# A decoder kernel: inverse softmax sums moved from VectorE to ScalarE in the first cross attention, weight scales moved into the linear attention

## What is computed

```python
x = x + gla(layernorm(x))
x = x + cross_attention(layernorm(x), ctx, ctx)      # the stage that is changed
x = x + attention_and_experts(layernorm(x))
x = x + t5_attention(layernorm(x)); x = x + similarity_attention(layernorm(x), ctx)
x = x + quantised_ffn(layernorm(x))                  # its weights are scaled by 127 / max|w|

# cross_attention: h = 16 heads, s = 77 keys
attn = softmax(einsum('bhtd,bhsd->bhts', q, k) * 8 ** -0.5)
out = einsum('bhts,bhsd->bhtd', attn, v).reshape(b, t, 128) @ out_w.T + out_b

# quantised_ffn, for each group of weights that share a scale
amax = clip(max(abs(w)), 1e-8); scale = 127 / amax
w_q = clip(round(w * scale), -128, 127) / scale
```

## Time and profile before

| what | us |
|---|---|
| median of 3 runs | 493.52 |
| the 3 runs | 493.2, 493.52, 498.61 |
| the profiled execution | 495.03 |
| span of the core in it | 493.2 |
| busy in the span: PE, DVE, ACT, POOL | 436.3, 373.3, 284.9, 212.8 |
| the cross attention, from the first scores to the last residual | 77.6 to 122.8 |

### The profile page before, as it was taken

The page is one execution under the profiler, slowest core; times in us unless marked ns, Lnnn a source line. Parts: engine busy times, 40 slices in busy tenths (PEclk is TensorE's granted clock), DMA queues, the critical chain, the costliest instruction groups (busy, mean ns, idle before and its releaser), DMA issues.

```text
span 493.2 us, 13018 instructions
## 1 busy us (share of the span) xinstructions
PE 436.3 (88%) x4488; PEld 303.9 (62%) x4488; DVE 373.3 (76%) x1005; ACT 284.9 (58%) x617; POOL 212.8 (43%) x542
## 2 busy tenths in 40 slices
PE   3879968887675899879999999999999998999897
PEld 1225555665573767746666676676676675887656
DVE  3746868998777699987777777778778777567666
ACT  2752324655328487567777777777777776413460
POOL 5050011270024265504685767667675776442200
PEclk9959988999999799999999999999999999999999
DMA  6388922600000012100000000000000000000001
GB/s 211 64 98 98 101 30 72 239 23 3 0 2 20 26 43 85 34 1 1 19 19 2 3 16 0 16 0 0 0 0 0 0 2 1 3 2 1 2 0 43
DMA packets 15619, 15.77 MB, mean 32 GB/s; under 512 B 1348, under 2 KB 12859, under 8 KB 15579
## 3 DMA queue, kind: packets, MB, share of 16 engines
q1 hardware_dynamic: 15579, 15.24, 15.1%
HBM read 10.52 MB, written 4.72 MB: 31 GB/s over the span
## 4 chain that ended last, share of the span: by engine, by line
PE 69%; DVE 22%; ACT 5%; issue 3%; DMA 1%; POOL 0%; SPq 0%; DVEq 0%; ACTq 0%; POOLq 0%
PE bank L922 16%; PE bank L1416 11%; PE bank L1368 9%; PE bank L1291 5%; PE bank L1218 4%; PE bank L1409 3%; PE bank L1205 3%; PE bank L1287 3%; PE bank L1306 2%; DVE PX L1716 2%; DVE mx L1714 2%; PE bank L1031 2%; PE bank L1528 1%; DVE stats L1555 1%; PE bank L1536 1%
## 5 line engine op out<-in xcount | busy, mean ns | idle before, releaser
L826 ACT ACTIVATE SN<-SN,nmx 128x512 f32<-128x512 f32 x128 | 92.7, 724 | 9.9 <-DVE nmx L1929 7.6
L922 PE MATMUL bank<-cs,SN 128*128 128x128 f32 x512 | 67.3, 274 | 3.3 <-DVE Z L1922 1.6
L922 PEld LDWEIGHTS bank<-cs,SN 128*128 128x128 f32 x512 | 57.1, 141 | 18.1 <-issue 12.1
L1368 PE MATMUL bank<-TK,TQ 64*128 64x512 f16 x384 | 52.6, 379 | 1.6 <-DVE TK L1892 1.6
L540 POOL TENSOR_TENSOR CTW<-YT 128x128 f32<-128x128 f32 x64 | 29.3, 458 | 51.5 <-DVE YT L1927 51.0
L1914 DVE CUSTOM_DVE_ANT_0 SN<-bank,strip 128x512 f32<-128x512 f32 x64 | 43.4, 677 | 1.2 <-PE bank L1368 0.6
L1929 DVE CUSTOM_DVE_ANT_0 SN<-bank,strip 128x512 f32<-128x512 f32 x64 | 43.6, 681 | 0.0
L1922 DVE COPY PTO<-bank 128x512 f32<-128x512 f32 x32 | 22.1, 692 | 21.0 <-PE bank L1416 20.9
L1922 DVE COPY Z<-bank 128x512 f32<-128x512 f32 x32 | 22.1, 691 | 16.0 <-PE bank L1416 15.9
L837 ACT COPY PTO<-bank 128x512 f32<-128x512 f32 x32 | 18.8, 586 | 26.1 <-PE bank L1416 26.1
L1416 PE MATMUL bank<-PTO,TV 128*64 128x128 f32 x512 | 33.4, 273 | 0.0
(11 more groups left out here) (314 smaller groups left out, 987.3 us busy)
## 6 DMA issues: line engine op xcount, KB each, us to landing
bias_rows<-biasr SPq DMA_DIRECT2D x1, 4096.0 KB, 44.4
band<-bias_rows SPq DMA_DIRECT2D x1, 3072.0 KB, 12.7
wqkv<-in_twqkv SPq DMA_DIRECT2D x8, 192.0 KB, 2.8
w1s<-in_w SPq DMA_DIRECT2D x8, 128.0 KB, 2.2
w2s<-in_w SPq DMA_DIRECT2D x8, 128.0 KB, 2.2
wB<-in_wb SPq DMA_DIRECT2D x1, 753.0 KB, 6.2
wA<-in_wa SPq DMA_DIRECT2D x1, 520.0 KB, 4.7
X<-in_x SPq DMA_DIRECT2D x2, 256.0 KB, 3.4
```

The costliest lines, as they stand in the source:

```text
L826: sc.activation(p, p, ACT.Exp, bias=nmx[:, r % RING, h:h + 1], scale=-1.0, accum_out=psm[:, r % RING, h:h + 1]).then_inc(sm["exp_ready"], 1)
L922: return nc.tensor.transpose(out_, in_, ident[0:n, 0:n])
L1368: ins = mm(bank[2 * (s % 2) + h][:, :], TQ[u][r, q_part, S * b + P * qt:S * b + P * qt + P], TK[u][r, k_part, S * b:S * b + S], start=(k = ...
```

## The change

Four edits. (1) The reciprocal of the sums leaves DVE. ACT makes it in a new function `inverse_sums(i)`: the logarithm of the sums from bank 6 into rc, then the exponential of minus that, which raises the new semaphore `rc_ready`. It is issued on ACT for tile i - 1 behind the exponential of tile i, and for tile 7 behind the loop, ahead of `rstd_of(3, 0)`. (2) The product that makes CT leaves its place ahead of `subtract_max(i + 1)` and stands inside it, between the maximum and the difference; the product of tile 6 stands behind the statistics of step 7, and that of tile 7 stays where it was. (3) `weight_scales` leaves the cross attention for the GLA loop, in three parts behind `gate_out` of tiles 0, 1 and 2, with its maximum split into two halves. (4) Semaphores `h1_mm` and `gl_mm` become one, `gk_mm`, counted on. What PE does, and in which order, is unchanged.

```diff
@@ -309,7 +309,7 @@
 
         names = """ld_x ld_cs ld_a ld_b ld_c ld_d bias_dma dve_c act_c qx_ready konst_ready
             ln_var ln_rstd ln_y ln_tp ln_yt x_done
-            qk_mm h1_mm h1_ready gl_mm u_ready l_ready g_ready e_ready kp_ready qs_ready kp_tp kpt_ready vg_mm vg_ready
+            qk_mm gk_mm h1_ready rc_ready u_ready l_ready g_ready e_ready kp_ready qs_ready kp_tp kpt_ready vg_mm vg_ready
             a_mm am_ready kv_mm st_ready o_mm ob_ready sq_ready ss_ready sr_ready og_ready ot_mm ot_ready go_mm
             kv_x_mm kb_ready kx_ready vx_ready vs_mm vb_ready qt_mm qt_hi qt_ready xb_ready s_mm px_sub px_ready pt_mm pt_ready xo_mm ct_ready ws_ready co_mm
             qkv_mm qkv_ready sc_ready se_ready at_pool at_ready att_mm att_ready pr_mm h2_ready rt_mm lg_ready le_ready xh_ready
@@ -627,7 +627,7 @@
                 take_yt(0, g)
 
             for g in range(NG):
-                act.wait_ge(sm["h1_mm"], g + 1)
+                act.wait_ge(sm["gk_mm"], g + 1)
                 sc.copy(H1[:, S * g:S * g + S], bank[4 + g][0:LR, :]).then_inc(sm["h1_ready"], 1)
             for g in range(NG):
                 c = slice(S * g, S * g + S)
@@ -701,9 +701,18 @@
             query_high(0)
             take_ot(1)
 
+            def inverse_sums(i):
+                act.wait_ge(sm["xo_mm"], i + 1)
+                if i >= 1:
+                    act.wait_ge(sm["ct_ready"], i)
+                link(sc.activation(rc[:, :], bank[6][:, P:2 * P], ACT.Ln))
+                sc.activation(rc[:, :], rc[:, :], ACT.Exp, scale=-1.0).then_inc(sm["rc_ready"], 1)
+
             for i in range(NT):
                 act.wait_ge(sm["px_sub"], i + 1)
                 sc.activation(PX[:, i % 2, :, :], PX[:, i % 2, :, :], ACT.Exp, scale=XD ** -0.5).then_inc(sm["px_ready"], 1)
+                if i >= 1:
+                    inverse_sums(i - 1)
                 if i == NT - 1:
                     rstd_of(2, 0)
                 if i == 1:
@@ -717,6 +726,7 @@
                         rstd_of(1, 1)
                     if i == 1 and c == 1:
                         query_high(1)
+            inverse_sums(NT - 1)
             rstd_of(3, 0)
 
 
@@ -952,10 +962,10 @@
             pe.wait_ge(sm["ld_a"], 48)
             for g in range(NG):
                 pe.wait_ge(sm["ln_yt"], g + 1)
-                mm(bank[4 + g][0:LR, :], wA_("gk1", LR), YT[:, S * g:S * g + S], start=True, stop=True).then_inc(sm["h1_mm"], 1)
+                mm(bank[4 + g][0:LR, :], wA_("gk1", LR), YT[:, S * g:S * g + S], start=True, stop=True).then_inc(sm["gk_mm"], 1)
             for g in range(NG):
                 pe.wait_ge(sm["h1_ready"], g + 1)
-                mm(bank[4 + g][:, :], wG2[:, :], H1[:, S * g:S * g + S], start=True, stop=True).then_inc(sm["gl_mm"], 1)
+                mm(bank[4 + g][:, :], wG2[:, :], H1[:, S * g:S * g + S], start=True, stop=True).then_inc(sm["gk_mm"], 1)
 
             pe.wait_ge(sm["ld_b"], 64)
             mm(bank[7][:, 0:NG * XS], wB_("in", P, P), wB_("ctxT", NG * XS), start=True, stop=True).then_inc(sm["kv_x_mm"], 1)
@@ -1586,7 +1596,7 @@
             norm(0, X, Y, lambda g: dve.wait_ge(sm["ld_x"], 32))
             dve.wait_ge(sm["ld_a"], 48)
             for g in range(NG):
-                dve.wait_ge(sm["gl_mm"], g + 1)
+                dve.wait_ge(sm["gk_mm"], NG + g + 1)
                 vv.tensor_scalar(U[:, S * g:S * g + S], bank[4 + g][:, :], col("gk_b"), None, ALU.add).then_inc(sm["u_ready"], 1)
 
             dve.wait_ge(sm["ld_b"], 64)
@@ -1680,6 +1690,18 @@
                 residual(g, X, 6, 0)
                 dve.wait_ge(sm["x_done"], g + 1)
 
+            def weight_scales(part):
+                if part < 2:
+                    dve.wait_ge(sm["ld_c"], 16)
+                    half = slice(FB * part, FB * part + FB)
+                    link(vv.tensor_reduce(amw[:, half], wC[:, F1 * part:F1 * part + F1].rearrange("p (j d) -> p j d", d=P), AX.X, ALU.max,
+                                          apply_absolute_value=True))
+                else:
+                    link(vv.tensor_scalar(amw[:, :], amw[:, :], 1e-8, None, ALU.max))
+                    link(vv.reciprocal(scw[:, :], amw[:, :]))
+                    link(vv.tensor_scalar(scw[:, :], scw[:, :], 127.0, None, ALU.mult))
+                    vv.tensor_scalar(inw[:, :], amw[:, :], 1 / 127.0, None, ALU.mult).then_inc(sm["ws_ready"], 1)
+
             gla_mask(0)
             for i in range(NT):
                 gla_state(i)
@@ -1687,6 +1709,8 @@
                     gla_mask(i + 1)
                 if i >= 1:
                     gate_out(i - 1)
+                if 1 <= i < TG:
+                    weight_scales(i - 1)
                 if i == TG:
                     head_sums(0)
                 if i == NT - 2:
@@ -1700,8 +1724,7 @@
             head_norm(1)
 
             def ctx_norm(i):
-                dve.wait_ge(sm["xo_mm"], i + 1)
-                link(vv.reciprocal(rc[:, :], bank[6][:, P:2 * P]))
+                dve.wait_ge(sm["rc_ready"], i + 1)
                 if i >= 2:
                     dve.wait_ge(sm["co_mm"], i - 1)
                 vv.tensor_tensor(CT[:, i % 2, :], bank[6][:, 0:P], rc[:, :], ALU.mult).then_inc(sm["ct_ready"], 1)
@@ -1712,21 +1735,13 @@
                 dve.wait_ge(sm["s_mm"], i + 1)
                 s4 = banks[:, 0:XH // HG, 0:GN].rearrange("p j (h s) -> p j h s", s=XS)
                 link(vv.tensor_reduce(mx[:, :].rearrange("p (j h) -> p j h", h=HG), s4, AX.X, ALU.max))
+                if i >= 2:
+                    ctx_norm(i - 2)
                 m = mx[:, :].rearrange("p (j h o) -> p j h o", h=HG, o=1).to_broadcast([P, XH // HG, HG, XS])
                 ins = vv.tensor_tensor(PX[:, i % 2, :, :].rearrange("p (j h) s -> p j h s", h=HG), s4, m, ALU.subtract)
                 ins.then_inc(sm["px_sub"], 1)
 
 
-
-            def weight_scales(part):
-                if part == 0:
-                    dve.wait_ge(sm["ld_c"], 16)
-                    link(vv.tensor_reduce(amw[:, :], wC[:, :].rearrange("p (j d) -> p j d", d=P), AX.X, ALU.max, apply_absolute_value=True))
-                    link(vv.tensor_scalar(amw[:, :], amw[:, :], 1e-8, None, ALU.max))
-                elif part == 1:
-                    link(vv.reciprocal(scw[:, :], amw[:, :]))
-                    link(vv.tensor_scalar(scw[:, :], scw[:, :], 127.0, None, ALU.mult))
-                    vv.tensor_scalar(inw[:, :], amw[:, :], 1 / 127.0, None, ALU.mult).then_inc(sm["ws_ready"], 1)
 
             def query_low(g):
 
@@ -1747,15 +1762,14 @@
                     dve.wait_ge(sm["co_mm"], TG)
                     dve.wait_ge(sm["xb_ready"], 1)
                     residual(0, XB, 7, 1)
-                if i >= 1:
-                    ctx_norm(i - 1)
+                if i == NT - 1:
+                    ctx_norm(NT - 2)
                 if i + 1 < NT:
                     subtract_max(i + 1)
                 if i == 0:
                     norm_rows(1, 1, X, Y)
                 if i == 1:
                     query_low(1)
-                weight_scales(i - 2)
             norm_rows(2, 0, X, Y)
             dve.wait_ge(sm["ln_y"], nth_norm(2, 0))
             norm_stats(3, 0, Y)
```

## The result

| | us |
|---|---|
| median before, 20 runs | 494.76 |
| median after, 20 runs | 497.16 (495.82 to 498.67) |
| ratio | 1.0042, 95% interval 1.0026 to 1.0057 |
| profiled execution after; its span | 496.55; 494.7 |

So the change costs 2.1 us (1.3 to 2.8). The forecast was +0.52 us, and its 494.0 with the range 490.2 to 496.2 stood on a median of three runs, which with 20 runs was 1.2 us higher. Carried over to 494.76, the forecast would have been 495.3. The mechanism of the stage came as forecast, but the forecast's +0.52 us is only a quarter of the measured cost; much of the rest of this document is about the other three quarters.

A forecast was written before the change was run, and what follows sets the result against it. The prediction took a cross-attention loop through PE and DVE as the bound, 5.10 us a tile after the change. Last residual +0.52, scales and clock nothing: 495.03 + 0.52 = 495.55, or 494.0 on the median's scale; range 490.2 to 496.2.

The forecast's parts named there:

- The loop over one tile: Cross attention: late product holds `ctx_o` ahead of piece 2 on PE; 5.10 us a tile, against 4.84 on average before.
- Step 7: Last tile of the cross attention: ACT's inverse sums delay the norm's pair, copies begin near 118.55 instead of 118.1, losing 0.4.
- The pair of ACT: Logarithm and exponential of the sums: 0.75 us with handovers, hidden in steps 1 to 6, bare behind the last tile.
- Behind 122.78 all work moves as one.: Everything after the cross attention's last residual shifts together, by the stage's +0.52 us.
- So I price the clock at nothing.: PE's new idle time of some 0.8 us per tile at `ctx_o` does not lower its clock: cost nothing.
- The base: Starting time: profiled execution 495.03 us, with the runs' median 493.52; on the median's scale the forecast is 494.0.
- The replay: Cross attention stepped through at 5.10 us a tile from R(1) = 91.90; last residual moves from 122.78 to 123.30.
- The scales in GLA: Three parts of the weight scales fit DVE's idle time in GLA to within 0.1 us; cost taken as nothing.
- The relief: Rival: `ctx_o` does not hold PE, the cross attention's loop is 4.4 us a tile, total 490.3; 14%.
- DVE's busy time: Rival: all 10.4 us taken off DVE comes off the time, giving 483.1, faster by 2.1%; 1%.
- table load: Rival: ACT's logarithm and exponential each load tables, 1.28 us each, about 10.5 more, giving 504.5; 3%.
- the fourth rival: GLA halves spill, ACT's pair holds the copies, or PE's longer idle pieces lower its clock: 496 to 502; 11%.

The follow-up runs named there:

- the first pair: The first traces of the kernel before and of the changed kernel: stage 44.46 against 45.18 us.
- the gaps behind the stage filled: Matmuls of ones added in PE's gaps between cross attention and first expert, in three kernels; ratios to before: change 1.0028, `ctx_o` behind piece 2 0.9961, before 1.0006.
- before's second trace: The kernel before run again unchanged for another trace: ratio 0.999 (0.9963 to 1.0017), stage 43.95 us.

## Why the prediction was wrong, step by step

- **The loop over one tile** (5.10 us): right. Measured 5.13 to 5.14, PE idle 0.89 at `ctx_o` with DVE as releaser (0.8 was forecast), product 1.47 behind the maximum. The run with `ctx_o` behind piece 2 shows that it is this order, by 3.2 us of stage.
- **Step 7**: right. ACT's pair and norm hold the copies; they start at 118.88 (118.55 was forecast). The end of the stage came at 123.50, forecast 123.30. The pair of ACT took 0.28 and 0.31, with the handovers 0.65 from 121.97 to the product at 122.62; I had 0.75. That the end fits to 0.2 is in part luck: ACT read the sums of tile 6 at 117.93 and not at 117.40, mostly by the late handover at 103.10, and a shorter step 7 and pair took some of it back.
- **"Behind 122.78 all work moves as one." and "So I price the clock at nothing."**: this is the step that failed, a term put at nothing. What the change costs beyond its stage is 0.9 to 1.4 of the 2.1 us. I had looked at PE's clock in the stage, where it is indeed 0.99 or 1.00 in every trace, and not at the gaps behind it, where a half-clock stretch can or can't occur. In the 13 traces of kernels in which nothing behind the stage differs, the way from the last residual to the first expert product is 28.4 us in 7 and 29.3 to 30.2 in 6, and the first expert takes 10.5, 11.0 or 11.9. All six long ones are of kernels with the inverse sums on ACT (6 of 9), none of the four with the reciprocal on DVE. The change, at its usual timing, gets more of these than before: 25 of 32 runs at 0.966, against 20 of 124 at 0.966 or less. An estimate from these: if such runs take 90.1 us from the last residual to the T5 scores and all others 88.1, the change is 1.2 slower than before there, which with the stage makes 1.9 to 2.4. It is an estimate only, since no execution of before at 0.966 was traced, and what part of the 2.1 us lies ahead of the first maximum, whose start varies by 2.4 us, no run separates.
- **The base**, the second term that failed. The replay ran against one execution of before. Its floor of the scales took 0.66, in three others of that order 0.48, 0.27 and 0.17. I used 0.66 only as a bound for GLA and did not ask whether it was usual. With 43.95 as the stage of before, the change costs 1.2 there, not the 0.72 of the first pair, and not 0.52. The range had another fault: it stood on a median of three runs, 493.52, where 20 runs have 494.76. With the same distances around 494.76 its upper end would have been 497.4, and 497.16 would have lain inside; the cost of the change would still have been mis-sized by the clock.
- **The scales in GLA**: right. The half maxima took 0.68, and the states keep their pace: 15.72 us from the one at 38.82 to the one at 54.54, in before 15.73 from 39.40 to 55.13. Alone this part shortens the stage by 0.7 to 1.2 us.
- **Rivals.** The relief did not come through, since `ctx_o` holds PE; it does when that is moved. DVE's busy time fell by 8.1 us and the time rose: to take work off the engine with the highest occupancy did not pay in this stage. No table load: the logarithm and exponential stand 0.31 apart. Of the fourth rival ("slower, within 2%", 11%), the time fell into its range and the clock took part, but where it expected PE's longer idle pieces in the stage to lower it, the drops lie behind the stage and their cause is open.

What is shown: the stage's cost and its cause; that the times behind the stage differ where half-clock stretches lie; that with the gaps behind the stage filled the two kernels are 1.1 us apart instead of 2.3. That these gaps are the whole of the rest is not shown, since the filling also brought a half-clock stretch near the end. What stays open: why the change has them so often. Half of PE's idle time in its stage was filled without removing them, and each kernel has its own usual clock. The two traces of the change have the same gaps up to the drop and differ by 0.32 us in when they come, so the place in time may matter; no run here moved the gaps and nothing else.

**A version that beats both.** The change with `ctx_o(i - 1)` behind piece 2: 0.9962 (0.9942 to 0.9982), or with the gaps filled 0.9961 (0.9940 to 0.9981). But the scales alone, with the reciprocal left on DVE, reach 0.997 (0.9952 to 0.9987), which can't be told from it: its stage is 1.24 longer (43.23 against 41.99), its way from the last residual to the T5 scores 1.04 shorter (88.32 against 89.36).

## What to carry to other kernels

Before work is taken off a full engine, write down what each consumer of the moved result has queued behind it on its own engine; here a product had a second customer on PE, and its place behind a maximum made a loop that cost more than the relief. Try the order of the consumer's queue together with the move: two exchanged lines on PE were worth 3.2 us of stage, the relief of DVE by the inverse sums without them nothing. For changes below half a percent, compare the stage in two traces of each kernel, and allow for the clock in later gaps to add or take as much again, as it did here.

## What the runs showed of the hardware

- TensorE's granted clock falls from the higher level (2.4 GHz, 1.00) to the lower (1.2 GHz, 0.50) mostly in or behind stretches in which PE is partly idle, and the code there does not decide it: in two executions of the changed kernel identical work took 28.40 us at a clock of 0.98 and 30.16 at 0.88, with the same gaps before the first difference. In the stage it stays at 0.99 or 1.00 with PE busy for 36 us of 45. The Trainium skill, page "TensorE: Matmul & The Clock Gate", section "What's actually happening", calls the cost of the ramp to the higher level run-variable and below 1% of a typical span. That agrees with the runs (from 28.40 to 30.16 us is 0.4% of the span, from 10.54 to 11.91 is 0.3%), but here it was as large as the effect under study.
- A half-clock stretch can cost nothing: in before's second trace the stretch behind the stage has a clock of 0.92 and still takes 28.40, since the slow matmuls are those of `keep_busy` (20 in 4.03 us instead of 2.40): the next transpose starts 0.6 later behind the residual, and the one after it, ahead of which PE had idled 0.49 for DVE, comes on time.
- The logarithm of 128x128 from PSUM took 0.26 to 0.28 us, less than the exponential of the same size from SBUF, 0.31; the reciprocal that they replace took 0.96 on DVE, three times a product of that size, 0.29.
- One small DVE instruction on 128x8, the floor of the scales, took 0.66 us in one execution of before and 0.17 in another, 0.48 and 0.27 in two kernels with the same DVE program. The three long ones ended within 0.03 us of a TENSOR_TENSOR on POOL (L468) that ran at the time (97.83 and 97.80 in the first); the cause was not tested.
